# Turning the gathered expert rows: transposes on TensorE with copies on ScalarE, instead of DMA transposes

## What is computed

```python
x = x + attention(layernorm(x), ctx, ctx, itok)         # 8 heads of 32, scores scaled with log(length)
x = x + moe(layernorm(x))

def moe(x):                                             # T = 2048 tokens, D = 512, 8 experts, top 2
    probs = softmax(xt @ gate_w); top_p, top_i = top_k(probs, 2)
    for k in range(2):
        # tokens are put into buf[e, pos], at most cap = 320 of each choice for one expert
        h = gelu(einsum('ecd,edf->ecf', buf, w1) + b1)  # F = 2048
        y = einsum('ecf,efd->ecd', h, w2) + b2 + gelu(buf @ wd) @ wu   # rank 32
        out += y[e, pos] * keep * top_p[:, k]
    return out + 0.2 * (gelu(xt @ sw1 + sb1) @ sw2 + sb2 + gelu(xt @ swd) @ swu)
```

## Time and profile before

| | |
|---|---|
| median of 3 runs | 1442.29 us (1440.14 to 1443.11) |
| profiled execution | 1442.29 us, span of its instructions 1440.5 us |
| mean granted TensorE clock | 0.99 of full speed |
| TensorE busy | 1364.7 us, 95% |
| VectorE busy | 775.1 us, 54% |
| ScalarE busy | 673.6 us, 47% |
| GpSimd busy | 233.2 us, 16% |
| DMA transposes | 80, median 5.5 us (eth) and 4.6 us (etl) from issue to landing |

### The profile page before, as it was taken

How to read it: one execution, slowest core, us unless ns; L and a number is a source line. 1 busy time by engine, 2 the same in 40 slices (tenths; PEclk the granted TensorE clock), 3 DMA queues, 4 the chain that set the end, 5 groups by cost and what they waited for, 6 DMA issues and landing times.

```text
span 1440.5 us, 27355 instructions
## 1 busy us (share of the span) xinstructions
PE 1364.7 (95%) x11412; PEld 976.2 (68%) x11476; DVE 775.1 (54%) x1281; ACT 673.6 (47%) x992; POOL 233.2 (16%) x219
## 2 busy tenths in 40 slices
PE   5788999999999999999699999999999999999995
PEld 2252737364554647375588888998888888888884
DVE  7885757575665757454352644527355362552610
ACT  4765655657565656563232533435244252442411
POOL 5820000000000000443100402104030040300202
PEclk9999999999999999999899999999999999999998
DMA  9413131312213032116734745547554564544402
GB/s 306 150 52 89 45 95 52 88 45 81 59 58 91 30 103 90 22 25 200 175 115 99 197 112 152 149 102 191 138 160 116 121 176 136 160 114 102 96 1 37
DMA packets 136732, 155.92 MB, mean 108 GB/s; under 512 B 59049, under 2 KB 79673, under 8 KB 136610
## 3 DMA queue, kind: packets, MB, share of 16 engines
q1 hardware_dynamic: 124322, 128.97, 30.1%
q0 software_dynamic: 12288, 25.21, 9.5%
HBM read 109.47 MB, written 34.15 MB: 100 GB/s over the span
## 4 chain that ended last, share of the span: by engine, by line
PE 86%; DVE 5%; DMA 2%; issue 2%; ACT 2%; SPq 1%; POOL 0%; POOLq 0%; DVEq 0%; ACTq 0%
PE banks L1627 24%; PE banks L1652 24%; PE banks L1546 10%; PE banks L1564 8%; PE banks L1493 8%; PE banks L1441 3%; PE banks L1473 3%; PE banks L1665 1%; DMA stage<-in_L_ffn_w 1%; SPq L754 1%; DVE rowmax L1121 1%; PE banks L1520 1%; PE banks L1532 1%; DVE rden L1138 1%; PE banks L1615 1%
## 5 line engine op out<-in xcount | busy, mean ns | idle before, releaser
L1652 PE MATMUL banks<-hidden,w2h 128*128 128x0 bf16 x2048 | 318.8, 275 | 0.0
L926 ACT ACTIVATE hidden<-banks,scales 128x512 f32<-128x512 f32 x256 | 171.4, 687 | 139.6 <-PE banks L1473 96.3
L1652 PEld LDWEIGHTS banks<-hidden,w2h 128*128 128x128 bf16 x2048 | 199.7, 98 | 30.3
L1121 DVE TENSOR_REDUCE rowmax<-banks 128x1 f32<-128x512 f32 x256 | 173.7, 685 | 69.7 <-PE banks L1441 69.4
L1652 PE MATMUL banks<-hidden,w2l 128*128 128x0 bf16 x1024 | 198.5, 276 | 0.0
L1010 ACT ACTIVATE hf<-banks,b1cols 128x640 f32<-128x640 f32 x128 | 101.7, 794 | 180.3 <-PE banks L1627 179.4
L1564 PE MATMUL banks<-w2h,hidden 128*128 128x512 bf16 x499 | 179.3, 379 | 1.3 <-issue 1.2
L1257 DVE TENSOR_TENSOR w1l<-stage,w1h 128x2048 bf16<-128x2048 f32 x32 | 73.4, 2292 | 189.2 <-ACT w1h L993 189.2
L1016 ACT ACTIVATE yT<-banks 128x640 f32<-128x640 f32 x32 | 22.5, 704 | 278.8 <-PE banks L1652 278.8
L1627 PE MATMUL banks<-eth,w1h 128*128 128x0 bf16 x1024 | 136.9, 277 | 0.0
L1627 PE MATMUL banks<-etl,w1h 128*128 128x0 bf16 x1024 | 136.3, 276 | 0.0
(11 more groups left out here) (178 smaller groups left out, 1915.9 us busy)
## 6 DMA issues: line engine op xcount, KB each, us to landing
stage<-in_L_ffn_w SPq DMA_DIRECT2D x64, 1024.0 KB, 5.5
split_parts<-hidden SPq DMA_DIRECT2D x16, 512.0 KB, 3.4
QS<-split_parts SPq DMA_DIRECT2D x48, 128.0 KB, 2.5
KS<-split_parts SPq DMA_DIRECT2D x48, 128.0 KB, 2.7
xin<-in_x SPq DMA_DIRECT2D x16, 256.0 KB, 3.0
cin<-in_ctx SPq DMA_DIRECT2D x16, 256.0 KB, 2.7
out_rows<-xin SPq DMA_DIRECT2D x16, 256.0 KB, 2.0
normed_rows<-x2r SPq DMA_DIRECT2D x16, 256.0 KB, 2.0
```

Of the source, the lines that this page charges most:

```text
L926: ac.activation(prob[n % NPH], bank(score_bank[unit]), ACT.Exp, scale=scales[:, g // 2:g // 2 + 1]).then_inc(s_exp, 1)
L1121: dv.reduce_max(rowmax[g % 2][:, i:i + 1], bank(score_bank[unit]), X_AXIS).then_inc(s_max, 1)
L1652: issued = mm(half_of(bank(b0 + j)).shape_from_register(bank_cols(e, j)), w[:, fb, rows], half_of(a[:, fb, :], j).shape_from_register(slot ...
```

## The change

The DMA transposes are removed from SyncE's program. A `turn_x` unit, at the same place in the list, is now eight bf16 transposes on TensorE (four column blocks of the high part and four of the low part) into one PSUM bank read as bf16, and two ScalarE copies from there to `eth` and `etl`. Expert 0 uses banks 4 and 5, the others 6 and 7, in turn by chunk. The semaphore `s_turned` is replaced by `s_et` (a chunk is transposed) and `s_etc` (two for each copied chunk): the next gather waits for `s_et`, `e_rank` for `s_etc`, a chunk's transposes for the copies of the chunk two before, and the first two `e_y` units for the copies of expert 0.

```diff
@@ sync_program
-                elif kind == "turn_x":
-                    _, e, c = unit
-                    if c == 0:
-                        sp.wait_ge(s_gather, 16 * CH * (e + 1))
-                    if e >= 2 and c == 0:
-                        sp.wait_ge(s_up, e_up_no(e - 2, FB - 1))
-                    for a, turned in enumerate((eth[e % 2], etl[e % 2])):
-                        dma(turned[:, :, c * P:c * P + P], xg[:, c, a * D:a * D + D], transpose=True).then_inc(s_turned, 16)
@@ pool_program, gather
-                        pool.wait_ge(s_turned, 16 * 2 * CH * e)
+                        pool.wait_ge(s_et, e * CH)
@@ act_program
+                elif kind == "turn_x":
+                    _, e, c = unit
+                    act.wait_ge(s_et, e * CH + c + 1)
+                    if e >= 2 and c == 0:
+                        act.wait_ge(s_up, e_up_no(e - 2, FB - 1))
+                    src = bank(E_TURN[e][c % 2]).bitcast(BF16).rearrange("p (a k t) -> p a k t", a=2, k=KB)
+                    n = 2 * (e * CH + c)
+                    ac.activation(eth[e % 2][:, :, c * P:c * P + P], src[:, 0], ACT.Copy).then_inc(s_etc, 1)
+                    ac.activation(etl[e % 2][:, :, c * P:c * P + P], src[:, 1], ACT.Copy).then_inc(s_etc, 1)
@@ banks
+        E_TURN = [(4, 5)] + [(6, 7)] * (E - 1)
@@ pe_program
+                elif kind == "turn_x":
+                    _, e, c = unit
+                    b = E_TURN[e][c % 2]
+                    if c == 0:
+                        pe.wait_ge(s_gather, 16 * CH * (e + 1))
+                    if e == 1 and c < 2:
+                        pe.wait_ge(s_y, GROUPS)
+                    elif c >= 2 or e > 1:
+                        pe.wait_ge(s_etc, 2 * (e * CH + c - 1) if c >= 2 else 2 * e * CH)
+                    view = bank(b).bitcast(BF16)
+                    for j in range(2 * KB):
+                        issued = tr(view[:, j * P:j * P + P], xg[:, c, j * P:j * P + P], identb[:, :])
+                    issued.then_inc(s_et, 1)
@@ e_rank
-                        pe.wait_ge(s_turned, 16 * 2 * CH * (e + 1))
+                        pe.wait_ge(s_etc, 2 * CH * (e + 1))
@@ e_y
                     if m >= 2:
                         pe.wait_ge(s_y, GROUPS + m - 1)
+                    else:
+                        pe.wait_ge(s_etc, 2 * CH)
```

More of the change, by code:

```diff
@@ L567, in build @@
         s_scatter, s_table, s_gather = sem("s_scatter"), sem("s_table"), sem("s_gather")
-        s_turned = sem("s_turned")
+        s_et, s_etc = sem("s_et"), sem("s_etc")
         s_ytc, s_yt = sem("s_ytc"), sem("s_yt")
```

## The result

The changed kernel took 1452.15 us as the median of four runs (1448.96 to 1455.62), the kernel before beside it 1442.6; the ratio is 1.0067, 95% interval 1.0045 to 1.0091, so 6.5 to 13 us more. The forecast was +4.5 us, 1446.8. The profiled execution was kinder than most: 1449.71 us, span 1446.6. The way and the range of 8 in 10 (1441.5 to 1456) hold. The middle is about 3 to 5 us short of the runs, and the median lies outside the forecast's own narrow range of 1444 to 1449; that is what the experiments had to find.

What follows compares the result with a forecast made beforehand. TensorE was taken to bound experts 1 to 7, with DMA transposes waited for only at the first expert. Transposes +15.6, first expert -9.1, clock -2.0 gave +4.5 us: 1446.8 us, 8-in-10 range 1441.5 to 1456.

Steps and rivals of the forecast that it cites:

- The cost on TensorE, 15.6 us: Experts 1 to 7: 40 added transposes each at 55.8 ns, all on the path; range 5.5 to 30.8 us.
- Rival C: TensorE transposes run at the pace of weight loads or f32 form, 98 to 110 ns: +20, 1462 us; chance 0.08.
- E: Transposes overlap in TensorE's array as the e_rank matmuls do, 19.6 ns each: -7.0, 1435.3 us; chance 0.08.
- 273 ns as a pace: The f32 transposes' duration taken as TensorE's pace for each transpose: +74, 1516 us; chance 0.02.
- Copies on ScalarE, cost 0 beside the downs: Experts 1 to 7: two PSUM copies per chunk, 6 us an expert, run beside the down matmuls in ScalarE's idle time.
- rival D: ScalarE's copies fall behind its splits and TensorE stops, 1.2 us in 7 experts: +8, about 1455 us; chance 0.06.
- SyncE's issues in experts 1 to 7 are worth 0: Removing DMA transposes from SyncE's queue there gains nothing, as TensorE has no idle they could have caused.
- The clock, -2.0 us: TensorE's clock no longer falls at the first expert: 0.78 us at e_rank plus 1.24 at the first e_up block.
- Expert 0, -9.1 us: First e_rank starts at about 690.4 instead of 699.49, expert 0's own transposes included.
- Rival B's second half: A slightly later gather, with one us of slack, stalls expert 0's chunk 0: 1 to 3 us more; whole rival's chance 0.12.
- signs of being wrong: Eight transposes over 0.6 or under 0.35 us, TensorE idle before a chunk, or first e_rank later than 693.

Runs made afterwards that it cites:

- rest_only: Against the kernel before: TensorE transposes for experts 1 to 7 only, DMA transposes kept for expert 0; 1456.8 us, ratio 1.0102.
- twice: The changed kernel with each transpose of experts 1 to 7 issued twice; 1469.3 us, ratio 1.0191 to the kernel before.
- mid_first: Against the kernel before: expert 0 alone on TensorE, chunk 0 after the 42nd of 48 steps, a chunk after each next step; 1431.4 us, ratio 0.9917.
- before_again: The kernel before, unchanged, run again for a second trace; 1442.05 us, ratio 0.9999.
- first_again: Against the kernel before: expert 0 alone on TensorE, chunks from the 33rd step on, repeated on another chip; 1433.2 us, ratio 0.9939.
- after: The changed kernel's first trace, all experts on TensorE; median 1452.15 us, ratio 1.0067 to the kernel before; profiled execution 1449.71 us.
- slow_before: The kernel before with twelve small fills on GpSimd ahead of expert 0's fifth gather; ratio 1.0000.
- first_only: Against the kernel before: TensorE transposes for expert 0 alone, experts 1 to 7 keep DMA transposes; 1435.9 us, ratio 0.9955.
- after_again: The changed kernel itself once more, for a second trace and more runs; 1449.1 us, ratio 1.0052 to the kernel before.
- before: The unchanged kernel with DMA transposes, in the trace the prediction read; profiled execution 1442.29 us.
- mid_all: The changed kernel with expert 0's chunk 0 after the 42nd of 48 steps, a chunk after each next; 1447.7 us, ratio 1.0039 to the kernel before.
- slow_after: The changed kernel with twelve small fills on GpSimd ahead of expert 0's fifth gather; ratio 1.0065 to the kernel before.
- late_first: Against the kernel before: expert 0 alone on TensorE, chunk 0 after the 43rd of 48 steps, a chunk after each following step; ratio 0.9961.
- late_all: The changed kernel with expert 0's chunk 0 after the 43rd of 48 steps, a chunk after each following step; ratio 1.0054 to the kernel before.
- The fills: Twelve small GpSimd fills, about 0.3 us each, ahead of expert 0's fifth gather; ratios 1.0000 in the kernel before, 1.0065 in the changed one against it.

## Why the prediction was right, and what it mis-sized

*The cost on TensorE, 15.6 us:* right. 55.9 ns against 55.8 from the matmul stream of the earlier trace rows; by the runs of rest_only 14.7 (12.4 to 16.9), with the runs of twice (20 for the second 280) as the one number that fits badly. Rival C (98 to 110 ns) and E (19.6) are out, as is 273 ns as a pace: the column shows 219 ns for the bf16 transposes while eight of them take 0.45 us.

*Copies on ScalarE, cost 0 beside the downs:* right. Experts 1 to 7 show no idle on TensorE; rival D did not come about. ScalarE is 42 us busier, not 48, since neighbouring copies overlap.

*SyncE's issues in experts 1 to 7 are worth 0:* right; from e_rank to e_rank nothing but the 2.2 us has changed.

*The clock, -2.0 us:* right, but again a sample. From the first to the last e_rank the kernel before has 1328.06 - 699.49 = 628.57 us and mid_first, with the same work there, 626.53: 2.04, and before_again against first_again gives 2.00. By the stretch from the first e_rank to the second, the fall cost only 1.3 us in rest_only (94.22 against 92.92 us in after) and 2.7 in slow_before (93.41 against 90.68 in first_only). It does not follow the length of the wait: 11.35 us cost 1.3, 8.18 us cost 2.7. In after_again the clock fell after all, inside the shared downs, behind the wait for the gather.

*Expert 0, -9.1 us:* the term that was mis-sized. Rival B's second half (a slightly later gather stalls chunk 0) had its cause, but with 1 to 3 us too small a price: against after, the three traces with a wait for the gather are 1.2, 3.2 and 6.1 us longer here. Two of the prediction's own signs of being wrong came in them: TensorE idle before a chunk, and a first e_rank later than 693 (695.6, 695.1 and 697.1; in twice the lateness of everything before it did the most of that). From the last group of the shared up pass to the first e_rank the traces have:

| | traces | mean |
|---|---|---|
| DMA transposes (before, before_again, rest_only) | 44.7, 41.5, 43.4 | 43.2 |
| TensorE, as changed (after, after_again, first_only, first_again, twice) | 35.5, 41.6, 38.7, 35.6, 36.7 | 37.6 |
| TensorE, place of mid (mid_first, mid_all) | 34.9, 34.9 | 34.9 |

The four traces of the chip with the stall are not in it. There slow_before has 43.3, no more than the others although TensorE was 3.0 us late; slow_after has 37.8, late_first 39.5 and late_all 39.3, all three with the stall of 2.5 to 2.7 us in them and the last two with the fall of the clock behind it.

The prediction compared 44.7 with 35.6, the widest pair of this table. The place of 35.6 was computed well (35.5 in the trace of the changed kernel, 35.6 in first_again). That this trace then followed the sum to the tenth was luck: it too had its gather in time, and was compared with the longest first wait seen. On average the part gives back 5.6 us, not 9.1: some 2 of the missing 3.5 are the wait for a held-up gather and what follows from it (37.6 against 35.5 where it was in time), 1.5 are the first wait of the kernel before, which is mostly shorter than in the one trace that was read. The sum then reads 15.6 - 5.6 - 2.0 = +8.0, and the runs have +7.5 and +9.7. It is an account after the fact, from eight traces on several chips. For the place of mid it is 15.6 - 8.3 - 2.0 = +5.3, and +5.6 was measured; without the seven experts -10.3 against -12.0 (-9.5 to -14.4). The medians of mid_all and after_again were taken on different chips and their intervals overlap; that the place alone makes the difference is shown by the waits in the traces, not by those two ratios.

*Open.* The part ahead of the experts, which the change doesn't touch, scatters by 4 us too: the last group of the shared up pass starts between 654.8 and 658.9 us in the ten traces, and 654.8 is the one of the prediction. How much of +7.5 or +9.7 comes from there is not shown. Why a gather instruction takes 3 us in some executions was not tried apart; the table shows only that it goes with weight loads that are issued faster, at a time when the DMA engines are fully busy. The fills show the one direction (a later gather, faster loads), not what makes the instruction long. The stall of 2.5 to 3.2 us ahead of the last shared downs, and a longer one some 25 us earlier, appeared in all four kernels of one chip and in none elsewhere; its cause is open. The first set of runs was 2 us further from the kernel before than the second; their intervals overlap, and the scatter of the gather or of the part ahead of the experts is enough to explain that, but no trace of those runs shows it.

## What to carry to other kernels

A wait that a single trace shows is a sample: before counting on its length, look at which queues' chains end there and how they compete, and ask what each chain would do if the other won. Moving work onto the busiest engine pays only where that engine was waiting for it: here for one expert in eight. Doing just that part gave -12.0 us where doing it everywhere, from the same place, cost 5.6; from the first place the two were -6.5 and +7.5. And when a step is taken from behind a late chain and put early, check how much room its other input had: one microsecond was too little, and nine steps later cost nothing in the traces.

## What was not expected of the hardware

An indirect gather's instruction on GpSimd took 1.0 us in five traces of ten and 2.4 to 3.1 us once or twice in the other five, and the last gather landed 7.7 to 9.7 us after its start instead of 6.0 to 6.1, always together with six 1 MB loads being issued in 18.8 to 20.6 us instead of 21.5 to 21.8. What the fall of TensorE's clock cost behind the first wait was 1.3, 2.0, 2.0 and 2.7 us in four traces, in no order of the waits' lengths. bf16 transposes of 128 x 128 ran at 55.9 ns start to start, the same as a matmul of 128 columns, with the granted clock at 1.00 in the windows of experts 1 to 7.
